# State-space chunks: the next chunk's x projected between the later exponent products, the last chunk's output projection behind them, and the convolution in one run

## The reference, cut to what matters

```python
def _mamba2(u, in_w, conv_w, conv_b, dt_bias, A_log, Dp, rms_w, out_w):
    zxbcdt = u @ in_w.T
    z, xBC, dt = jnp.split(zxbcdt, [D_INNER, D_INNER + CONV_DIM], axis=-1)
    dt = jax.nn.softplus(dt + dt_bias)
    xBC = conv_general_dilated(xBC, conv_w, ...)      # depthwise, 4 taps, over the tokens
    xBC = jax.nn.silu(xBC + conv_b)
    xh, Bm, Cm = jnp.split(xBC, ...)                  # 32 heads of 32, state of 32
    dA = jnp.exp(dt * -jnp.exp(A_log))
    # per token: state = dA*state + (dt*x) B^T ; y = state . C
    y = y + Dp * xh
    y = y * jax.nn.silu(z)
    y = y * rsqrt(mean(y * y, -1) + EPS) * rms_w
    return y @ out_w.T
# twice: h = h + _mamba2(_layernorm(h), ...)
```

## Time and profile before

| | |
|---|---|
| median of 3 runs | 1711.53 us (1709.33 to 1713.68) |
| the profiled execution: its time, its span | 1710.17 us, 1708.4 us |
| mean granted TensorE clock | 0.871 of full speed |
| busy share of the span: TensorE, weight load, VectorE, ScalarE, GpSimd | 80%, 54%, 65%, 39%, 24% |
| first L1033 of the two layers | 173.62 and 517.00 us |
| one middle chunk, 382.59 to 417.59: busy TensorE, VectorE, ScalarE, GpSimd | 30.80, 28.05, 15.00, 14.43 of 35.00 us |

### The profile page before, as it was taken

How to read it: one execution, slowest core, us unless ns; L and a number is a source line. 1 busy time by engine, 2 the same in 40 slices (tenths; PEclk the granted TensorE clock), 3 DMA queues, 4 the chain that set the end, 5 groups by cost and what they waited for, 6 DMA issues and landing times.

```text
span 1708.4 us, 34435 instructions
## 1 busy us (share of the span) xinstructions
PE 1363.5 (80%) x12846; PEld 928.9 (54%) x12847; DVE 1109.4 (65%) x1669; ACT 671.5 (39%) x1011; POOL 417.0 (24%) x390
## 2 busy tenths in 40 slices
PE   3734889888548989884738999976699999999991
PEld 2214566665345666652425555544477777777770
DVE  3586877887578778876876555556456774667432
ACT  3236434344364343341252111124346664566330
POOL 0122333443313434432132323323100000000004
PEclk9757799999778899987858999885799999999996
DMA  8051000000220000003221000005543553535004
GB/s 293 18 173 61 2 2 1 1 1 1 80 82 2 2 1 1 1 1 105 93 83 50 0 0 0 0 4 209 193 183 142 218 217 114 218 126 219 25 25 153
DMA packets 34029, 132.30 MB, mean 77 GB/s; under 512 B 6665, under 2 KB 8457, under 8 KB 24017
## 3 DMA queue, kind: packets, MB, share of 16 engines
q1 hardware_dynamic: 25808, 103.19, 16.7%
q0 software_dynamic: 8160, 28.32, 4.9%
HBM read 108.82 MB, written 22.68 MB: 77 GB/s over the span
## 4 chain that ended last, share of the span: by engine, by line
PE 57%; DVE 24%; issue 7%; ACT 6%; DMA 4%; POOL 2%; DVEq 0%; POOLq 0%; SPq 0%; ACTq 0%
PE banks L2102 13%; PE banks L2123 13%; DVE mb_ca L592 8%; PE banks L1644 6%; PE banks L1003 5%; PE banks L1721 2%; PE banks L977 2%; PE banks L1040 2%; PE banks L1697 2%; PE banks L1050 2%; PE banks L1051 1%; ACT mb_ca L804 1%; POOL xs_table L2135 1%; DVE mb_xc L604 1%; DVE mb_y_lo L640 1%
## 5 line engine op out<-in xcount | busy, mean ns | idle before, releaser
L2102 PE MATMUL banks<-eb_x_hi,eb_w_hi 128*128 128x128 f16 x1344 | 228.3, 220 | 2.0 <-DVE eb_x_lo L2002 2.0
L2102 PE MATMUL banks<-eb_x_lo,eb_w_hi 128*128 128x128 f16 x1344 | 228.3, 220 | 0.0
L2102 PE MATMUL banks<-eb_x_hi,eb_w_lo 128*128 128x128 f16 x1344 | 228.3, 220 | 0.0
L977 PE MATMUL banks<-mb_u_hi,mb_wi_hi 128*128 (+3 forms) x1152 | 198.0, 220 | 3.3 <-ACT mb_ca L804 3.3
L977 PE MATMUL banks<-mb_u_hi,mb_wi_lo 128*128 (+3 forms) x1152 | 197.7, 220 | 0.0
L977 PE MATMUL banks<-mb_u_lo,mb_wi_hi 128*128 (+3 forms) x1152 | 197.6, 220 | 0.0
L592 DVE SCALAR_TENSOR_TENSOR mb_ca<-mb_xp,mb_par,mb_ca 128x128 f32<-128x128 f32 x384 | 162.9, 487 | 25.3 <-ACT mb_ca L804 23.3
L2102 PEld LDWEIGHTS banks<-eb_x_hi,eb_w_hi 128*128 128x128 f16 x1344 | 132.3, 98 | 4.8 <-issue 2.4
L2102 PEld LDWEIGHTS banks<-eb_x_lo,eb_w_hi 128*128 128x128 f16 x1344 | 132.3, 98 | 2.4
L2102 PEld LDWEIGHTS banks<-eb_x_hi,eb_w_lo 128*128 128x128 f16 x1344 | 132.3, 98 | 0.0
L2123 PE MATMUL banks<-eb_w_hi,eb_h_hi 128*128 x336 | 127.9, 381 | 0.4 <-issue 0.4
(11 more groups left out here) (431 smaller groups left out, 3255.0 us busy)
## 6 DMA issues: line engine op xcount, KB each, us to landing
eb_raw<-e_w SPq DMA_DIRECT2D x36, 1024.0 KB, 4.8
eb_un<-e_w SPq DMA_DIRECT2D x28, 1024.0 KB, 7.2
mb_ring<-m_in_w SPq DMA_DIRECT2D x8, 1072.0 KB, 5.4
xs_table<-zero POOLq DMA_DIRECT2D x1, 6400.0 KB, 21.0
eb_xg<-xs_table POOLq DMA_DIRECT2D x23, 256.0 KB, 2.9
ys_table<-eb_y POOLq DMA_DIRECT2D x21, 256.0 KB, 6.5
ab_raw<-a_in_w SPq DMA_DIRECT2D x4, 1154.0 KB, 11.8
mb_ring<-m_out_w SPq DMA_DIRECT2D x4, 1024.0 KB, 5.3
```

The costliest lines, as they stand in the source:

```text
L977: x = e.matmul(ps[0:width, bank, n * P:(n + 1) * P], a[:, k, f:f + width], b[:, k, ds(i * P, P)], start=(k == 0 and m == 0), stop=(k == KD ...
L2102: o = e.matmul(ps[:, j, c * P:(c + 1) * P], a[:, side, k, f * P:(f + 1) * P], b[:, k, :], start=(k == 0 and m == 0), stop=(k == KD - 1 and ...
```

## The change

On TensorE, in every chunk but the last of a layer, the four places behind the exponent products take a quarter of the next chunk's x projection each (24 matmuls), the first of which waits for the gate `sz_done`; B and C follow behind the loop; the last chunk's output projection stands behind them in one run of 24 matmuls, and the sum of squares behind that. On VectorE the 24 taps stand in one run, the row norm comes behind them, the row update and the product with the state between the two halves of x, the next state behind B and C, and the row statistics behind the gated y. On ScalarE the decay exponential stands between the tanh of x's two halves. No instruction is added or taken away in a middle chunk, and GpSimd's and SyncE's lists are as they were.

```diff
-            def conv(g, after_half=None, inside=None, after_x=None):
+            def conv(g, after_taps=None, between=None):
...
-                        if q == 1 and k == 0 and inside:
-                            inside()
                     x.then_inc(acc, 1)
-                    if q == 0 and after_half:
-                        after_half()
+                if after_taps:
+                    after_taps()
...
-                    if q == 0 and after_x:
-                        after_x()
+                    if q == 0 and between:
+                        between()
...
-                if not is_first:
-                    row_norm(g - 1)
...
+                def last_rows():
+                    if not is_first:
+                        add_rows(i - 1, g - 1)
+                    from_state()
+
                 if is_last:
-                    add_rows(i - 1, g - 1)
-                    from_state()
-                    next_state()
+                    row_norm(g - 1)
+                    last_rows()
                 else:
                     e.wait_ge(dx_done, g + 1)
-                    conv(g + 1, None if is_first else lambda: add_rows(i - 1, g - 1), from_state, next_state)
-                if not is_first:
-                    row_stats(i - 1, g - 1)
+                    conv(g + 1, None if is_first else lambda: row_norm(g - 1), last_rows)
+                next_state()
...
                 e.tensor_tensor(y, y, sz[:], ALU.mult).then_inc(y_done, 1)
+                if not is_first:
+                    row_stats(i - 1, g - 1)
...
-                else:
-                    grow(g - 1)
                 for q in range(2):
+                    if q == 1 and not is_first:
+                        grow(g - 1)
                     e.wait_ge(acc, 2 * g + q + 1)
...
+            def project_x(i, n):
+                project(i, n // 2, [MB_CX + P * j for j in (2 * n, 2 * n + 1)], P, x_mm if n % 2 else None, n % 2 * 2)
...
-                    if k >= 4 and not is_first:
-                        out_project(g - 1, 2 * (k - 4), 2 * (k - 3))
...
+                    if k >= 4 and not is_last:
+                        if k == 4:
+                            e.wait_ge(sz_done, 2 * (g + 1))
+                            core.apart(e)
+                        project_x(i + 1, k - 4)
+                if not is_last:
+                    project_bc(i + 1, g + 1)
+                if not is_first:
+                    out_project(g - 1)
                     e.wait_ge(m_done, MB_EG * (g + 1))
                     sum_rows(g - 1)
-
-                if is_last:
-                    last_rows()
-                else:
-                    project_x(i + 1, g + 1, False, None if is_first else last_rows)
                 e.wait_ge(exped, MB_EG * (g + 1))
```

More of the change, by code:

```diff
@@ L971, in pe, with project @@
             x.then_inc(dt_mm, 1)
-            def project(i, bank, tiles, width, done):
-                for n, f in enumerate(tiles):
+            def project(i, bank, tiles, width, done, at=0):
+                for n, f in enumerate(tiles, at):
                     for k in range(KD):
@@ L978, in project, with project_bc @@
                                          b[:, k, ds(i * P, P)], start=(k == 0 and m == 0), stop=(k == KD - 1 and m == 2))
-                x.then_inc(done, 1)
-            def project_x(i, g, is_first, rows=None):
-                if not is_first:
-                    e.wait_ge(sz_done, 2 * g)
-                for q in range(2):
-                    project(i, q, [MB_CX + P * j for j in range(4 * q, 4 * q + 4)], P, x_mm)
-                    if q == 0 and rows:
-                        rows()
+                if done:
+                    x.then_inc(done, 1)
+            def project_x(i, n):
+                project(i, n // 2, [MB_CX + P * j for j in (2 * n, 2 * n + 1)], P, x_mm if n % 2 else None, n % 2 * 2)
+            def project_bc(i, g):
                 e.wait_ge(x_ev, 2 * g + 1)
@@ L996, in project_z, with out_project @@
                 project(i, 0, [P * j for j in range(4, 8)], P, z_mm)
-            def out_project(g, first, end):
+            def out_project(g):
                 e.wait_ge(ylo_done, g + 1)
-                for j in range(first, end):
+                for j in range(JD):
                     for m, (a, b) in enumerate(((y_hi, wo_hi), (y_hi, wo_lo), (y_lo, wo_hi))):
@@ L1004, in out_project @@
                                      stop=(j == JD - 1 and m == 2))
-                if end == JD:
-                    x.then_inc(out_mm, 1)
+                x.then_inc(out_mm, 1)
             def sum_rows(g):
@@ L1011, in sum_rows @@
                 e.matmul(ps[:, 2, 384:385], ysq[:, 0, :], core.ones[:, 0:1], start=True, stop=True).then_inc(rms_mm, 1)
-            project_x(0, l * TT, True)
+            for n in range(4):
+                project_x(0, n)
+            project_bc(0, l * TT)
             e.wait_ge(la_done, l + 1)
@@ L1052, in body @@
                         .then_inc(diff, 1)
-                    if k >= 4 and not is_first:
-                        out_project(g - 1, 2 * (k - 4), 2 * (k - 3))
-                def last_rows():
+                    if k >= 4 and not is_last:
[7 more added lines that the diff above has]
+                    out_project(g - 1)
                     e.wait_ge(m_done, MB_EG * (g + 1))
                     sum_rows(g - 1)
-                if is_last:
-                    last_rows()
-                else:
-                    project_x(i + 1, g + 1, False, None if is_first else last_rows)
                 e.wait_ge(exped, MB_EG * (g + 1))
@@ L1091, in pe @@
             chunks(e, l, body)
-            out_project(l * TT + TT - 1, 0, JD)
+            out_project(l * TT + TT - 1)
             sum_rows(l * TT + TT - 1)
```

## The result

| | before | after |
|---|---|---|
| median, us | 1710.43 (1708.32 to 1713.68, 4 runs) | 1661.65 (1659.57 to 1666.38, 4 runs) |
| ratio, 95% interval | | 0.9713 (0.9691 to 0.9735) |
| span of the profiled execution | 1708.4 | 1658.7 |
| mean granted TensorE clock | 0.871 | 0.891 |
| first L1033 to the end of the last gated y, layer 1 / layer 2 | 267.0 / 267.2 | 243.8 / 244.3 |

The change gained 48.8 us; I had forecast some 30, with 1668 as the lower end. The direction was right, the size not.

What follows compares the result with a forecast made beforehand. VectorE was taken to close the 35.8 us middle chunks, TensorE to end them at 32.9 after the change. Middle chunks -29.0, those behind first chunks -4.2, first +2.0, last +0.8: -30.4 us, to 1681, range 1668 to 1696.

Steps and rivals of the forecast that it cites:

- What bounds the kernel: Middle chunks of the state-space stage: VectorE closes the 35.8 us chunk before; after the change TensorE ends it at 32.9.
- I keep 5.7: Middle chunk: fifth exponent product stays at t = 5.7, as warm TensorE and VectorE's later first L658 nearly cancel.
- The size of the cold start: The two chunks behind a first chunk still start with a cold TensorE, about +0.8: -2.1 us, twice.
- Steps, taps, evictions: Middle chunk: a step takes 1.78 us, 24 taps 7.0, evicting x's first half 2.0; L1066 starts at t = 21.3.
- The port: Middle chunk: GpSimd holds VectorE's L609 until t = 29.8 and the gated y for 1.3 us; output sums end at 32.2.
- The first and the last chunk: In each of two layers, the first chunk changes by +1 us and the last by +0.4.
- The sum: All chunks together: -29.0 - 4.2 + 2.0 + 0.8 = -30.4 us, giving 1681.
- The first (the port is free, 1670): L609 and L700 are not held by GpSimd; exponents come 0.7 to 0.9 us earlier, 1670; chance 0.17.
- The second: VectorE and GpSimd still close the middle chunk, at 34.1 us; total 1695; chance 0.11.
- the fourth: The new order gives nothing, as something else waits ahead of the taps; within 5 us of 1711; chance 0.03.
- The third: TensorE's clock falls inside the chunk, 2.1 us a fall: 1706 for one, 1733 for two; chance 0.03 each.
- My limit for it: TensorE's idle time beyond which the clock falls: somewhere between 0.79 and 2.31 us.

Runs made afterwards that it cites:

- the early eviction: The changed kernel, with ScalarE evicting the first half of x between its seventh and eighth exponential instead of behind the eighth: 1651.46 us, ratio 0.9660.
- the ten added products: The kernel before, with ten matmuls of unused result added in TensorE's idle time ahead of a chunk: 1688.72 us, ratio 0.9871.

## Why the prediction was wrong, step by step

**What bounds the kernel.** Right: VectorE closed the chunk before, TensorE does now, with no idleness ahead of it from a layer's third chunk on. That the edits only work together was not in the prediction: with TensorE's old list 1713, with its new list alone 1751. It also missed how much of the gain is the clock's. A middle chunk went from 35.7 us on average to 31.6. The kernel before with a warm TensorE and all its orders unchanged is at 33.9, which is 1.8 of these 4.1 us.

**"A warm TensorE would be earlier, VectorE's first L658 will be later (below); the two nearly cancel, and I keep 5.7."** This step failed. It measured 4.62. The warm clock is worth 1.2 us in the very chunk I had costed (4.55 with the orders of before), and VectorE's delay, as it came out, is worth 0.0, since y's high half on ScalarE covers it: 0.5 us less of the delay moved the fifth exponent product by 0.01. The delay was mis-sized besides: VectorE's gate ended at t = 3.26, not 3.8. That matters, because the cover is thin. With the early eviction the first decay product starts 0.35 us later (3.54), and the fifth exponent product follows by 0.34 (4.96). By these rows a delay of the forecast's size would have given some 5.1 (an estimate: 4.96 and the 0.18 by which 3.8 lies behind the gate's end there, 3.62), still not 5.7. I had put a number to one of two terms of opposite sign (VectorE's 1.3 us), none to the other, and let them cancel. That VectorE had room stood in the trace of before, in ScalarE's timeline:

```profile
386.74 1.05 ACT L835 ACTIVATE mb_y_hi<-mb_quad 128x1024 f16<-128x1024 f32 x1
387.69 1.08 ACT L851 ACTIVATE mb_E<-banks 128x512 f32<-128x512 f32 x2
```

The third exponential follows y's high half at 387.69, 1.0 us after VectorE's first decay product was done (386.71).

**The size of the cold start.** I priced it at "about +0.8" for the chunks behind a first chunk. These were not cold at all (idle 0.83 and 0.0 us ahead of them): 31.6 us, forecast 33.7, which is 4.2 us over two. And the cold start alone, taken away from the kernel before, made the twelve chunks between a layer's first and last 22.1 us shorter, 1.8 each; the two last chunks, which were warmed as well, gained nothing (45.8 us together, 45.7 before).

**Steps, taps, evictions.** Right to 0.1: from the fifth exponent product on, one step after the other took 1.86, 1.78 and 1.77 us (1.78), 24 taps in 6.89 (7.0), L1066 6.8 us behind the start of B and C (6.9), 11.6 us from there to the last z product (11.6).

**The port.** L607 was held by L942 (2.11, forecast some 2), as said. L699 took 1.94 to 2.02, forecast 2.4: I had given the faded state 2.53 us, but that row held a wait for VectorE's own instruction; alone L929 takes 1.90. VectorE's own end of the chunk was forecast at 32.2 and came at 31.03, so the slack to TensorE was 0.6, where 0.7 was forecast: both sides are early by the same term.

**The first and the last chunk.** A first chunk was forecast at +1; it measured +1.0 and +2.8. Its convolution of B and C does fall among the taps, as said (24 taps in 9.48 us). The last was forecast at +0.4 and measured +0.7 and -0.5. The two layers run the same lists here and have the same idle times, 1.32 and 1.76 us in the first chunk, 0.82 and 1.13 in the last. They differ in TensorE's clock. Windows of the first chunks (t = 20 to 27, layer 1 and layer 2) and of the whole last chunks:

```profile
192.50:199.50 7.00, 6.63 (x123) 5.21 (x124) 6.93 (x15) 1.35 (x4) 2.82 (x4) 1.00 0.01 2
512.60:519.60 7.00, 6.58 (x70) 3.40 (x71) 6.93 (x15) 1.30 (x3) 2.82 (x4) 0.55 0.01 2
392.50:416.25 23.75, 18.69 (x147) 9.83 (x145) 17.21 (x23) 8.06 (x13) 7.58 (x7) 0.93 0.09 28
714.67:736.89 22.22, 17.18 (x147) 9.36 (x145) 17.21 (x23) 8.07 (x13) 7.57 (x7) 1.00 0.07 15
```

So the clock did fall within a chunk of the changed kernel, once in a first and once in a last one, for 2.1 and 1.5 us. Where it stayed whole, the first chunk measured +1.0, the forecast's value, and the last -0.5. That the +1.0 agrees is luck: I had taken it between bounds of -2.9 and +2.34.

**The sum.** From the forecast's -30.4: the ten middle chunks 12.1 more (1.1 each for the fifth exponent product, the rest smaller), the two behind a first chunk 4.8 more, first and last 1.3 less, and 3.6 outside the stage, which was no part of it and lies within the scatter given above: -49.6.

**The rivals.** The first (the port is free, 1670) came nearest in time, for the wrong reason: the holds are there, and cost nothing in this kernel, where TensorE does not wait for VectorE at a chunk's start. The second and the fourth did not occur. The third did not occur in the middle chunks, but did in one first and one last chunk, and does in the middle chunks of two neighbours of this change. A fall cost 1.7 us in the first of these, where I had put 2.1. My limit for it, between 0.79 and 2.31 us of idleness, does not hold: the clock fell behind 1.32 and 0.44 us, stayed whole behind the same two, and stayed whole behind 3.06 us (last section).

## What to carry to other kernels

When two engines' lists are permuted together, test the halves in the head: each alone can lose what both gain. Price a cold TensorE from several stretches, not from one, and never let two effects of opposite sign cancel without a row for each; ask of each which of the two waits ends last. And when a step is moved later, follow not only its readers but what is queued behind them: the square moved for ScalarE's sake cost more through GpSimd's queue than it gained. Before a difference between two chunks is put down to an order or a hold, compare TensorE's clock in both: here equal chunks with equal idle times differ by 1.5 to 2 us through the clock alone.

## What the runs showed of the hardware

- The length of an idle time alone did not decide TensorE's clock. Within a chunk, 0.82 and 1.32 us left it at 1.00 in all twelve chunks of the changed kernel between a layer's first and last. With TensorE's old list, 1.32 and 0.44 us close together were followed by 0.50 in seven of ten middle chunks and left it at 1.00 in three. With its new list alone, 2.3 us were followed by a fall in seven of twelve chunks. Ahead of a chunk, 1.0 to 1.35 us left it whole with the ten added products, and 2.1 to 2.2 us with TensorE's new list alone. In the kernel with L941 behind the halo, 3.06 us ahead of layer 1's second chunk left it at 1.00, and 3.05 us at the same place in layer 2 were followed by 0.50 over 4.31 us. The idle times ahead of the chunks of the kernel before (a layer's first left out), 2.3 and 3.2 to 3.3 us, were each followed by 0.50 to 0.62 over 4.31 us.
- The wait of VectorE for GpSimd ended, in L607, L699, L604, L609 and L638, with one instruction of GpSimd's (2.34 or 1.9 us). When L928 followed L943 without a pause, L604 still got in between. The Trainium skill, page "SBUF — State Buffer", section "SBUF: two separate sides", describes the shared port pair as a lock held for one instruction; these five agree. The tap of 3.20 us, which outlasted the end of one instruction of GpSimd's and all of the next, remains the exception, and no run here explains it. With TensorE's new list alone the same tap has only L941 beside it (2.36 us), and takes 2.48: one instruction again. So I had generalised the odd case.
- Where taps and GpSimd's convolution run together, 24 taps take 9.5 us instead of 6.9: 9.48 in the changed kernel's first chunks, 9.47 in the middle chunks of the kernel with B and C's convolution ahead of the power.
